# Reading and turning x inside the first expert's program, on one Trainium2 core

## The chip, the core and the metric

The kernel runs on one core of a Trainium2 chip. Its engines are TensorE (PE in the profile; PEld is its weight load), VectorE (DVE), ScalarE (ACT), GpSimd (POOL) and SyncE (SP). SP and ACT can both issue DMAs, each into a queue of its own (q1 is SP's, q10 is ACT's); the core's 16 DMA engines serve both. The metric is the device time of one launch in microseconds.

## What is computed

The program is a chain of four blocks on x (32 sequences of 64 tokens, width 256, so N = 2048 tokens): a gated sum over nine SwiGLU experts, an attention on that sum, five routed experts with two shared ones, and a second attention with four routed experts. The change touches the start of the first block alone. Cut to that block:

```python
# h = x; E, D, F = 8, 256, 1024; g are gating probabilities, Sg, Su, Sd the shared expert
g = jnp.einsum('bsd,edf->ebsf', h, Wg)
u = jnp.einsum('bsd,edf->ebsf', h, Wu)
expert_outs = jnp.einsum('ebsf,efd->ebsd', jax.nn.silu(g) * u, Wd)
# result: shared gate * shared expert + (1 - shared gate) * sum over e of gate[e] * expert_outs[e]
```

## The kernel before, in words

**Two programs.** `load_inputs` is a program of its own with a block of instructions for each engine. SP loads the table of constants (`const`, whose first 128 columns are the identity), x in four quarters into `x_tok`, and six small inputs with many tiny rows (`load_small`: gates, types, a bias, a threshold). ACT issues the first expert's weights: gate and up (`stage_up`, 1 MB each) and down (`stage_dn`, 1 MB). PE turns x: tokens lie in the partitions of `x_tok`, features in those of `xT`; 32 transposes of 128x128 go through the eight PSUM banks, four to a bank. ACT writes the rounded copy `x_hi`, DVE (and for every second bank ACT) the plain copy `xT`, DVE the remainder `x_lo = x - x_hi`. POOL sets the sum `sumT` to zero. At the end DVE waits for the small inputs and prepares the gates (`not_shared` L2039 to `type_sel` L2049). Then `sem.give_back()` clears the semaphores and all engines meet at a barrier. Only then comes `ffn`.

**The expert program.** `ffn` runs nine experts over four tiles of 512 tokens (`TT` = 4) and eight slices of 128 hidden features (`FC` = 8), so an expert has 32 steps (`STEPS`), counted by `st`. The first expert is written out, those between run in a loop on every engine. For a step PE does an up step (`up_step`, L269, here called U0, U1, ...: gate and up, 12 matmuls of 128x512) and a down step (`down_step`, L285, here D0, D1, ...: 6 matmuls). PE runs U two steps ahead: U0, U1, then U2, D0, U3, D1 and so on. Every product is made of three matmuls on rounded parts (hi*hi, hi*lo, lo*hi), so weights are split too: ACT rounds a slice (`round_up` L318, `round_down` L326), POOL subtracts (`cond_w_lo` L239, `cond_d_lo` L245). For the first expert ACT rounds all eight slices of up and then all eight of down before it does anything else.

**Between U and D.** ACT computes `silu` (L337), DVE multiplies it into `h` (L406), ACT rounds `h` one step later (`h_hi`, L331), DVE makes the remainder `h_lo` (L377). D of step st needs that `h_lo` and the down slice. Two pairs of banks (0 to 3) hold the products of U, banks 4 to 7 the sums of D, 6 and 7 from the second token tile on. After each token tile DVE's `take` multiplies the sum by the gate into `part` and adds it to `sumT` (L394, L397). Hooks of a `Beside` object let other work join; here `WeightsBeside` only adds the loads and the split of the next block's weights late in the program.

**Queues.** Every engine runs its own instructions strictly in order, and waits are on semaphores. SP issues the next expert's weights when all eight slices of `w_lo` (then of `d_lo`) are made.

Of the kernel before, what the change touches and what calls it, by code (L numbers as in the profile page):

```python
# [27 lines left out]
SLOT = 256  # L28

# [57 lines left out]
class ExpertStage:  # L87


    def __init__(self, nc, ctx, tag, ups):  # L90
        self.up = ctx.enter_context(nc.sbuf_tensor(f"{tag}_stage_up", [P, ups, KC, F], F32))
        self.down = ctx.enter_context(nc.sbuf_tensor(f"{tag}_stage_dn", [P, FC, D], F32))
        self.up_loaded = ctx.enter_context(nc.semaphore(f"{tag}_up_loaded"))
        self.dn_loaded = ctx.enter_context(nc.semaphore(f"{tag}_dn_loaded"))

    def load_up(self, sp, sources):
        for j, src in enumerate(sources):
            sp.dma_start(self.up[:, j], src).then_inc(self.up_loaded, 16)

# [4 lines left out]
class Beside:  # L104


    def sync_early(self, sp):
        pass
# [19 lines left out]
    def sync_late(self, sp):  # L128
        pass


class WeightsBeside(Beside):


    def __init__(self, weights):
        self.sync_late, self.scalar_late, self.gpsimd_late = weights.load, weights.round, weights.split
# [35 lines left out]
def ffn(nc, m, tag, swiglu, groups, gate, targets, x_hi, x_lo, stage, beside):  # L172
# [19 lines left out]
    with ExitStack() as s:  # L192
# [16 lines left out]
        with nc.Block() as block:  # L209
# [21 lines left out]
            def _(pool):  # L231
                def split(e):
# [14 lines left out]
                split(0)  # L247
                if n == 2:
# [7 lines left out]
            def _(pe):  # L256
# [31 lines left out]

                for st in range(2):
                    up_step(0, st)  # L290
                def expert(e, first):
                    for st in range(STEPS):
                        if first and st == FC:
# [16 lines left out]
            def _(act):  # L310
                def round_up(e, i):


                    if i == 0:
# [18 lines left out]
                def expert(e, first, last):  # L333
                    for st in range(STEPS):
# [30 lines left out]
            def _(dve):  # L365
# [4 lines left out]
                dve.nop().then_inc(gated, 2 * KC)  # L370

# [11 lines left out]
                def take(e, tt, target):  # L383
# [3 lines left out]
                    for c in range(KC):  # L387
# [4 lines left out]
                        if not (isinstance(e, int) and e == 0 and tt == 0):  # L392
                            dve.wait_ge(summed, KC * (TT * e + tt - 1) + c + 1)
# [5 lines left out]
                def expert(e, first, target, before):  # L399
                    for st in range(STEPS):  # L400
# [11 lines left out]
                        else:  # L412
                            split(e, st)
                        if first and st == FC + 1:
# [1558 lines left out]
def load_inputs(nc, m, x, x_hi, x_lo, stage, up, down):  # L1973

    sem = StageSemaphores(nc, "load")
    const_loaded, turned, taken, rounded = sem("const_loaded"), sem("x_turned"), sem("x_taken"), sem("x_rounded")
    small_loaded, gated, copied = sem("small_loaded"), sem("gated"), sem("x_copied")
    QT = 4
    x_loaded = [sem(f"x_loaded{q}") for q in range(QT)]
    with ExitStack() as s:  # L1980
        x_tok = s.enter_context(nc.sbuf_tensor("x_tok", [P, NP, D], F32))
        BANKS = 8
        with nc.Block() as block:
            @block.sync
            def _(sp):
                sp.dma_start(m.const[:], m.consts_dram).then_inc(const_loaded, 16)
                rows = x.rearrange("b t d -> (b t) d").rearrange("(i p) d -> p i d", p=P)
                for q in range(QT):
                    i = slice(q * NP // QT, (q + 1) * NP // QT)
                    sp.dma_start(x_tok[:, i], rows[:, i]).then_inc(x_loaded[q], 16)  # L1990
                m.load_small(sp, small_loaded)

            @block.gpsimd
            def _(pool):
                pool.memset(m.sumT[:], 0.0)
                pool.memset(m.minus_one[:], -1.0)
                pool.memset(m.zero_row[:], 0.0)

            @block.tensor
            def _(pe):  # L2000
                pe.wait_ge(const_loaded, 16)
                for i in range(NP // 2):
                    if i % 2 == 0:
                        pe.wait_ge(x_loaded[i // 2], 16)
                    if i >= BANKS:
                        pe.wait_ge(taken, i - BANKS + 1)
                    for j in range(2):
                        for c in range(KC):
                            ins = pe.transpose(m.bank[i % BANKS][:, (c * 2 + j) * P:(c * 2 + j + 1) * P],
                                               x_tok[:, 2 * i + j, c * P:(c + 1) * P], m.ident)  # L2010
                    ins.then_inc(turned, 1)

            @block.scalar
            def _(act):
                stage.load_up(act, up)
                stage.load_down(act, down)
                for i in range(NP // 2):
                    tok = slice(i * 2 * P, (i + 1) * 2 * P)
                    bank = m.bank[i % BANKS].rearrange("p (c t) -> p c t", c=KC)
                    act.wait_ge(turned, i + 1)  # L2020
                    act.activation(x_hi[:, :, tok], bank, ACT.Copy).then_inc(rounded, 1)
                    if i % 2 == 1:
# [187 lines left out]
```

## Time and profile before

| | |
|---|---|
| runs of the kernel | 2348.88 us median of 3 (2348.33 to 2353.54) |
| the profiled execution | 2349.1 us, of it a span of 2347.3 us from the first instruction to the last |
| mean granted TensorE clock | 0.943 of full speed |
| PE busy in the span | 2109.5 us, 90% |
| ACT / DVE / POOL busy | 907.1 / 1223.0 / 764.7 us |
| first matmul of the experts | at 40.82 us |
| last matmul of the ninth expert | at 1226.03 us |
| DMA moved | 135.74 MB, 58 GB/s over the span |

A row of the timeline gives the start, the duration, the engine, line, operation, destination and sources of one instruction or of several alike in a row (xN); in brackets how long the engine had been idle before it, and whose work ended that idle time. Times of a stretch are microseconds from the start of the span. A granted clock of 1.00 is 2.4 GHz on TensorE, 0.50 is 1.2 GHz.

### The profile page before, as it was taken

Reading aid. Unit: us, or ns where it says so; the run is one execution under the profiler, and the core shown is the slowest. Engines: PE = TensorE matmul, PEld = TensorE weight load, DVE = VectorE, ACT = ScalarE, POOL = GpSimd, SP = SyncE. Lnnn points to the kernel's source line nnn. Section 1 sums busy time; section 2 is a strip of 40 time slices with the busy share of each in tenths; the row PEclk is TensorE's granted clock in tenths of the full one; section 3 lists DMA queues with packets and bytes.
Section 4 is the critical chain, followed back from the end, with each engine's and each line's share of the span. In section 5 each row is a group of like instructions: output and inputs, shape, how many; then the busy total and the mean of one; then the engine's idle time right before and its main releaser. Section 6 shows DMA issues by size and latency. Waiting matters only on the chain. (4 is left out here: it accounts for less than half of the span.)

```text
span 2347.3 us, 32471 instructions
## 1 busy us (share of the span) xinstructions
PE 2109.5 (90%) x11748; PEld 1791.1 (76%) x11748; DVE 1223.0 (52%) x1989; ACT 907.1 (39%) x1780; POOL 764.7 (33%) x844
## 2 busy tenths in 40 slices
PE   3999999999999999999988797999897468967998
PEld 2888888888888888888877676788797157847997
DVE  2343344433344334443348894423784866657886
ACT  3233332324232332324222696132553223445554
POOL 3021020303020110203003595020783475507885
PEclk7999999999999999999997798999998688978999
DMA  3001010101001010200003002200463031036661
GB/s 124 30 0 55 1 54 0 54 0 47 7 2 51 0 54 0 78 0 0 1 1 72 24 37 102 94 9 1 154 198 97 18 72 40 38 107 225 206 202 58
DMA packets 84957, 135.74 MB, mean 58 GB/s; under 512 B 9678, under 2 KB 63312, under 8 KB 84880
## 3 DMA queue, kind: packets, MB, share of 16 engines
q1 hardware_dynamic: 78368, 118.72, 15.8%
q0 software_dynamic: 4928, 12.86, 1.6%
q10 hardware_dynamic: 1584, 3.15, 0.4%
q8 instruction: 47, 0.77, 0.1%
q14 instruction: 30, 0.25, 0.0%
HBM read 106.91 MB, written 12.06 MB: 51 GB/s over the span
## 5 line engine op out<-in xcount | busy, mean ns | idle before, releaser
L406 DVE TENSOR_TENSOR cond_h<-cond_silu,ps 128x512 f32<-128x512 f32 x288 | 197.9, 687 | 712.6 <-ACT cond_silu L337 709.0
L337 ACT ACTIVATE cond_silu<-ps 128x512 f32<-128x512 f32 x288 | 172.2, 598 | 793.7 <-PE ps L269 793.7
L269 PE MATMUL ps<-a_x_hi,cond_w_hi 128*128 128x512 f32 x1152 | 450.3, 391 | 20.6 <-POOL cond_w_lo L239 20.6
L269 PE MATMUL ps<-a_x_lo,cond_w_hi 128*128 128x512 f32 x1152 | 450.0, 391 | 0.0
L269 PE MATMUL ps<-a_x_hi,cond_w_lo 128*128 128x512 f32 x1152 | 449.8, 390 | 0.0
L239 POOL TENSOR_TENSOR cond_w_lo<-cond_stage_up,cond_w_hi 128x256 fp32r<-128x256 f32 x144 | 108.1, 771 | 869.4 <-ACT cond_w_hi L318 869.4
L269 PEld LDWEIGHTS ps<-a_x_hi,cond_w_hi 128*128 128x128 f32 x1152 | 217.3, 189 | 66.0 <-POOL cond_w_lo L239 20.8
L269 PEld LDWEIGHTS ps<-a_x_lo,cond_w_hi 128*128 128x128 f32 x1152 | 217.3, 189 | 45.1
L269 PEld LDWEIGHTS ps<-a_x_hi,cond_w_lo 128*128 128x128 f32 x1152 | 217.2, 189 | 45.1
L285 PE MATMUL ps<-cond_h_hi,cond_d_hi 128*128 128x512 f32 x576 | 224.8, 390 | 5.3 <-POOL cond_d_lo L245 4.5
L285 PE MATMUL ps<-cond_h_hi,cond_d_lo 128*128 128x512 f32 x576 | 224.8, 390 | 0.0
L285 PE MATMUL ps<-cond_h_lo,cond_d_hi 128*128 128x512 f32 x576 | 224.7, 390 | 0.0
L377 DVE TENSOR_TENSOR cond_h_lo<-cond_h,cond_h_hi 128x512 fp32r<-128x512 f32 x288 | 202.9, 705 | 0.1
L331 ACT ACTIVATE cond_h_hi<-cond_h 128x512 fp32r<-128x512 f32 x288 | 179.7, 624 | 0.3 <-DVE cond_h L406 0.3
L285 PEld LDWEIGHTS ps<-cond_h_hi,cond_d_hi 128*128 128x128 f32 x576 | 108.3, 188 | 28.5 <-POOL cond_d_lo L245 4.9
L1678 POOL TENSOR_TENSOR moe_w_lo<-moe_stage_up,moe_w_hi 128x512 fp32r<-128x512 f32 x88 | 114.9, 1321 | 38.6 <-ACT moe_w_hi L1779 37.8
L285 PEld LDWEIGHTS ps<-cond_h_hi,cond_d_lo 128*128 128x128 f32 x576 | 108.3, 188 | 22.5
L285 PEld LDWEIGHTS ps<-cond_h_lo,cond_d_hi 128*128 128x128 f32 x576 | 108.3, 188 | 22.4
L1731 PE MATMUL ps<-moe_x_hi,moe_w_hi 128*128 128x256 f32 x352 | 101.3, 288 | 13.9 <-DVE moe_x_lo L1832 13.9
L380 DVE SCALAR_TENSOR_TENSOR dense_h_lo<-ps,dense_h_hi 128x512 fp32r<-128x512 f32 x64 | 44.2, 692 | 122.6 <-ACT dense_h_hi L343 122.6
L1678 POOL TENSOR_TENSOR typed_w_lo<-typed_stage_up,typed_w_hi 128x256 fp32r<-128x256 f32 x88 | 69.0, 804 | 97.5 <-ACT typed_w_hi L1779 96.7
L1731 PE MATMUL ps<-moe_x_lo,moe_w_hi 128*128 128x256 f32 x352 | 100.7, 286 | 0.0
(357 smaller groups left out, 4396.7 us busy)
## 6 DMA issues: line engine op xcount, KB each, us to landing
moe_stage_up<-in_L_ffn_expert_wv SPq DMA_DIRECT2D x22, 1024.0 KB, 8.8
typed_stage_up<-in_L_cond_wi SPq DMA_DIRECT2D x11, 1024.0 KB, 5.0
typed_stage_dn<-in_L_cond_wo SPq DMA_DIRECT2D x11, 1024.0 KB, 5.4
moe_stage_dn<-in_L_ffn_expert_proj SPq DMA_DIRECT2D x11, 1024.0 KB, 5.6
cond_stage_up<-in_L_cond_Wg SPq DMA_DIRECT2D x7, 1024.0 KB, 4.9
cond_stage_up<-in_L_cond_Wu SPq DMA_DIRECT2D x7, 1024.0 KB, 7.0
cond_stage_dn<-in_L_cond_Wd SPq DMA_DIRECT2D x7, 1024.0 KB, 5.3
hyp_v_now<-hyp_v_blk SPq DMA_DIRECT2D x16, 272.0 KB, 2.3
```

What stands on the lines that cost most here:

```text
L239: ins = pool.tensor_tensor(w_lo[:, j, :, c], stage_up[:, j, :, c], w_hi[:, j, :, c], ALU.subtract)
L269: ins = pe.matmul(up_ps[st % 2][j], w[:, j, k, fs], x[:, k, tok], start=(i == 0), stop=(i == 3 * KC - 1))
L285: ins = pe.matmul(y_ps[tt % 2][c], w[:, f, cs], x[:, st % HB], start=(f == 0 and i == 0), stop=(f == FC - 1 and i == 2))
L331: act.activation(h_hi[:, st % HB], h[:, st % 2], ACT.Copy).then_inc(h_rounded, 1)
L337: act.activation(silu[:, st % 2], up_ps[st % 2][0], ACT.Silu).then_inc(act_done, 1)
L377: dve.tensor_tensor(h_lo[:, st % HB], h[:, st % 2], h_hi[:, st % HB], ALU.subtract).then_inc(h_ready, 1)
L380: dve.scalar_tensor_tensor(h_lo[:, st % HB], up_ps[st % 2][0], 0.0, h_hi[:, st % HB], ALU.max, ALU.subtract).then_inc(h_ready, 1)
L406: dve.tensor_tensor(h[:, st % 2], silu[:, st % 2], up_ps[st % 2][1], ALU.mult).then_inc(up_free, 1)
L1678: pool.tensor_tensor(w_lo[:, :, :, fs(f)], stage_up[:, q, :, :, fs(f)], w_hi[:, :, :, fs(f)], ALU.subtract).then_inc(up_ready, 1)
L1731: ins = pe.matmul(up_ps[f % UB][j], w[:, j, k, fs(f)], x[:, q, k], start=(i == 0), stop=(i == 3 * KC - 1))
```

## The change

`load_inputs` is gone as a program. Its work hangs on the hooks of `ffn` as `StartBeside`:

- SP loads the identity alone, the four quarters of x, the rest of the constants, then the small inputs. The raw rows of x lie in the memory of `sumT`, which nobody else needs yet.
- ACT issues the weights in five pieces: gate and up of the first two slices (`HEAD` = 2), their other six slices, down.
- PE turns the first quarter of x, waits until its copies are made, and starts with U0. The other three quarters are turned ahead of U3, U5 and U7 (steps 1, 3, 5), always through banks 6 and 7. ACT and DVE do their copies of a quarter in the same steps.
- For the first expert ACT rounds slice 0 of up, does its part of the first quarter, rounds slices 1 and 2, and rounds the rest one slice of up and one of down in each of the first steps.
- `sumT` isn't set to zero as a whole: the first expert's `take` writes it (one DVE operation in place of two), and only its last quarter is cleared by POOL, since that quarter is taken in the loop. The gates are prepared by DVE in step 9.
- One clearing of semaphores with its barrier goes with `load_inputs`.

```diff
+    def sync_early(self, sp):
+        m = self.m
+        sp.dma_start(m.const[:, 0:P], m.consts_dram[:, 0:P]).then_inc(self.ident_loaded, 16)
+        for q in range(self.QT):
+            i = slice(q * NP // self.QT, (q + 1) * NP // self.QT)
+            sp.dma_start(self.x_tok[:, i], self.rows[:, i]).then_inc(self.x_loaded[q], 16)
+        sp.dma_start(m.const[:, P:], m.consts_dram[:, P:]).then_inc(self.const_loaded, 16)
+        m.load_small(sp, self.small_loaded)
+    def scalar_start(self, act):
+        self.stage.load_up_head(act, self.up)
+        self.stage.load_up_rest(act, self.up)
+        self.stage.load_down(act, self.down)
+    def gpsimd_clear(self, pool):
+        pool.wait_ge(self.turned, NP // 2)
+        for c in range(KC):
+            pool.memset(self.m.sumT[:, c, N - TW:], 0.0).then_inc(self.cleared, 1)
+    def tensor_tile(self, pe, t):
+        if t == 0:
+            pe.wait_ge(self.ident_loaded, 16)
+        pe.wait_ge(self.x_loaded[t], 16)
+        for i in range(2 * t, 2 * t + 2):
+            bank, _ = self.place(i)
+            if i >= 2:
+                pe.wait_ge(self.taken, i - 1)
+            for j in range(2):
+                for c in range(KC):
+                    ins = pe.transpose(bank[:, c, j * P:(j + 1) * P], self.x_tok[:, 2 * i + j, c * P:(c + 1) * P], self.m.ident)
+            ins.then_inc(self.turned, 1)
+    def tensor_ready(self, pe, t):
+        pe.wait_ge(self.taken, 2 * (t + 1))
+    def scalar_tile(self, act, t):
+        for i in range(2 * t, 2 * t + 2):
+            bank, tok = self.place(i)
+            act.wait_ge(self.turned, i + 1)
+            act.activation(self.x_hi[:, :, tok], bank, ACT.Copy).then_inc(self.rounded, 1)
+            if i % 2 == 1:
+                act.activation(self.m.xT[:, :, tok], bank, ACT.Copy).then_inc(self.copied, 1)
...
@@ (PE, ffn)
+                beside.tensor_tile(pe, 0)
+                beside.tensor_ready(pe, 0)
                 for st in range(2):
                     up_step(0, st)
                 def expert(e, first):
                     for st in range(STEPS):
+                        if first and st in (1, 3, 5):
+                            beside.tensor_tile(pe, (st + 1) // 2)
+                        if first and st % FC == FC - 2 and st + 2 < STEPS:
+                            beside.tensor_ready(pe, (st + 2) // FC)
...
@@ (ACT, ffn)
+                        if first and beside.paced:
+                            if st + HEAD + 1 < FC:
+                                round_up(0, st + HEAD + 1)
+                            if st < FC:
+                                round_down(0, st)
+                            if st in (1, 3, 5):
+                                beside.scalar_tile(act, (st + 1) // 2)
...
-                for i in range(FC):
-                    round_up(0, i)
-                for i in range(FC):
-                    round_down(0, i)
+                beside.scalar_start(act)
+                if beside.paced:
+                    round_up(0, 0)
+                    beside.scalar_tile(act, 0)
+                    for i in range(1, HEAD + 1):
+                        round_up(0, i)
...
@@ (DVE, ffn, take)
-                        if not (isinstance(e, int) and e == 0 and tt == 0):
-                            dve.wait_ge(summed, KC * (TT * e + tt - 1) + c + 1)
+                        if isinstance(e, int) and e == 0:
+                            dve.tensor_tensor(target[:, c, tok].rearrange(v, t=T), y_ps[tt % 2][c].rearrange(v, t=T),
+                                              gate(e, tt), ALU.mult).then_inc(gated, 1)
+                            continue
+                        dve.wait_ge(summed, KC * (TT * e + tt - 1) + c + 1)
```

`vector_tile` is DVE's counterpart of `scalar_tile`: it copies the even bank into `xT` and subtracts for `x_lo`, as in `load_inputs`; step 31 of DVE waits for POOL's clearing.

## Rows read from the trace of the kernel before

**Rows 1.** Timeline, the first 41 us: start us, us, engine, line, operation.
```profile
1.18 6.71 SPq L1990 DMA_DIRECT2D x_tok<-in_x  x4
...
11.57 1.94 PE L2009 MATMUL ps<-const,x_tok 128*128 128x128 f32 x8 [11.57 <-DMA x_tok<-in_x]
...
13.93 1.50 DVE L2035 TENSOR_TENSOR a_x_lo<-ps,a_x_hi 128x512 fp32r<-128x512 f32 x2
14.04 0.59 ACT L2023 ACTIVATE xT<-ps 128x512 f32<-128x512 f32 x1
...
17.08 3.13 PE L2009 MATMUL ps<-const,x_tok 128*128 128x128 f32 x16 [0.57 <-DMA x_tok<-in_x]
...
36.30 0.18 DVE L2039 TENSOR_SCALAR not_shared<-gate_cond 128x32 f32<-128x32 f32 x1 [13.54 <-DMA threshold<-in_L_attn_threshold]
...
38.55 5.01 ACT L318 ACTIVATE cond_w_hi<-cond_stage_up 128x256 fp32r<-128x256 f32 x16 [16.90 <-PEq L84]
39.35 5.55 POOL L239 TENSOR_TENSOR cond_w_lo<-cond_stage_up,cond_w_hi 128x256 fp32r<-128x256 f32 x8 [34.84 <-ACT cond_w_hi L318]
...
40.82 0.79 PE L269 MATMUL ps<-a_x_hi,cond_w_hi 128*128 128x512 f32 x1 [20.61 <-POOL cond_w_lo L239]
```

**Rows 2.** Timeline, 50 to 96 us, the first down steps.
```profile
50.08 0.69 DVE L406 TENSOR_TENSOR cond_h<-cond_silu,ps 128x512 f32<-128x512 f32 x1 [1.36 <-ACT cond_silu L337]
...
50.68 5.81 DVE L377 TENSOR_TENSOR cond_h_lo<-cond_h,cond_h_hi 128x512 fp32r<-128x512 f32 x1
...
53.18 2.76 POOL L245 TENSOR_TENSOR cond_d_lo<-cond_stage_dn,cond_d_hi 128x256 fp32r<-128x256 f32 x4
...
56.59 0.47 PE L285 MATMUL ps<-cond_h_hi,cond_d_hi 128*128 128x512 f32 x1 [4.54 <-POOL cond_d_lo L245]
...
62.40 0.39 PE L285 MATMUL ps<-cond_h_hi,cond_d_hi 128*128 128x512 f32 x1
...
95.04 0.39 PE L285 MATMUL ps<-cond_h_hi,cond_d_hi 128*128 128x512 f32 x1
```

**Rows 3.** Windows of 1 us: busy time per engine, then PEclk, DMA share, GB/s.
```profile
46.00:47.00 1.00, 1.00 (x4) 0.77 (x4) 0.00 (x0) 0.98 (x2) 1.00 (x3) 0.60 0.00 0
...
57.00:58.00 1.00, 1.00 (x4) 0.76 (x3) 0.82 (x2) 0.00 (x0) 0.00 (x0) 0.52 1.01 406
...
60.00:61.00 1.00, 1.00 (x4) 0.80 (x4) 0.00 (x0) 0.00 (x0) 0.00 (x0) 0.77 1.00 367
```

**Rows 4.** DMA view by stretch: 0 to 5, 5 to 10 and 20 to 36.3 us.
```profile
DMA packets 278, 0.99 MB, mean 198 GB/s; under 512 B 16, under 2 KB 16, under 8 KB 278
...
DMA packets 859, 2.01 MB, mean 402 GB/s; under 512 B 31, under 2 KB 481, under 8 KB 859
...
q10 hardware_dynamic: 450, 1.59, 78.4%
q1 hardware_dynamic: 409, 0.42, 23.9%
...
q1 hardware_dynamic: 1975, 0.01, 5.5%
```

**Rows 5.** Transposes by source line (ns min/median/max), and windows over two of them.
```profile
L2009 PE MATMUL ps<-const,x_tok x32: 272/421/477, 11.6 to 19.9; 128*128 128x128 f32 x32
...
L1920 PE MATMUL ps<-const,c_back_y x32: 420/422/473, 1806.5 to 1814.5; 128*128 128x128 f32 x32
...
1445.50:1449.10 3.60, 3.47 (x32) 3.48 (x32) 2.39 (x3) 3.49 (x5) 0.00 (x0) 1.00 0.50 196
...
1810.00:1812.00 2.00, 2.00 (x11) 2.00 (x10) 0.00 (x0) 1.09 (x2) 0.00 (x0) 0.50 1.09 357
...
11.00:12.00 1.00, 0.43 (x2) 0.46 (x3) 0.00 (x0) 0.00 (x0) 0.00 (x0) 1.00 1.09 350
```

**Rows 6.** Timeline of one step in which the next expert's weights are split.
```profile
161.82 0.69 DVE L377 TENSOR_TENSOR cond_h_lo<-cond_h,cond_h_hi 128x512 fp32r<-128x512 f32 x1
...
162.32 1.48 POOL L239 TENSOR_TENSOR cond_w_lo<-cond_stage_up,cond_w_hi 128x256 fp32r<-128x256 f32 x2 [2.60 <-ACT cond_w_hi L318]
```

More of the change, by code:

```diff
@@ L104, with gpsimd_start, tensor_left, vector_tile @@
 class Beside:
+    paced = False
     def sync_early(self, sp):
+        pass
+    def scalar_start(self, act):
+        pass
+    def gpsimd_start(self, pool):
+        pass
+    def tensor_tile(self, pe, t):
+        pass
+    def tensor_ready(self, pe, t):
+        pass
+    def tensor_left(self, pe):
+        pass
+    def scalar_tile(self, act, t):
+        pass
+    def vector_tile(self, dve, t):
+        pass
+    def gpsimd_clear(self, pool):
+        pass
+    def vector_cleared(self, dve):
         pass
@@ L231, in _ @@
             def _(pool):
+                beside.gpsimd_start(pool)
                 def split(e):
@@ L247, in _ @@
                 split(0)
+                beside.gpsimd_clear(pool)
                 if n == 2:
@@ L292, in expert @@
                     for st in range(STEPS):
+                        if first and st in (1, 3, 5):
+                            beside.tensor_tile(pe, (st + 1) // 2)
+                        if first and st % FC == FC - 2 and st + 2 < STEPS:
+                            beside.tensor_ready(pe, (st + 2) // FC)
+                        if first and st == FC:
+                            beside.tensor_left(pe)
                         if first and st == FC:
@@ L311, in round_up @@
                 def round_up(e, i):
-                    if i == 0:
+                    if beside.paced and isinstance(e, int) and e == 0:
+                        if i == 0:
+                            act.wait_ge(stage.head_loaded, 16 * ups)
+                        elif i == HEAD:
+                            act.wait_ge(up_loaded, 16 * ups)
+                    elif i == 0:
                         act.wait_ge(up_loaded, 16 * ups * (e + 1))
@@ L370, in _ @@
                 dve.nop().then_inc(gated, 2 * KC)
+                if gate is not None:
+                    dve.nop().then_inc(summed, KC * (TT - 1))
+                beside.vector_tile(dve, 0)
                 def split(e, st, offset=0):
@@ L413, in expert @@
                             split(e, st)
+                        if first and st in (1, 3, 5):
+                            beside.vector_tile(dve, (st + 1) // 2)
+                        if first and st == STEPS - 1:
+                            beside.vector_cleared(dve)
                         if first and st == FC + 1:
@@ L2114, in program @@
                 sg, su, sd = one(a["L0_cond_Sg"]), one(a["L0_cond_Su"]), one(a["L0_cond_Sd"])
-                load_inputs(nc, m, a["x"], x_hi, x_lo, stage, (up(wg)(0), up(wu)(0)), down(wd)(0))
+                start = StartBeside(nc, m, s, a["x"], x_hi, x_lo, stage, (up(wg)(0), up(wu)(0)), down(wd)(0), hyp)
                 groups = [(E_COND, lambda e: (up(wg)(e), up(wu)(e)), down(wd)),
@@ L2119, in program @@
                     "p o b -> p (o b)").unsqueeze(2).to_broadcast([P, BT, T])
-                ffn(nc, m, "cond", True, groups, gate, [m.sumT, m.sumT], x_hi, x_lo, stage, WeightsBeside(hyp))
+                ffn(nc, m, "cond", True, groups, gate, [m.sumT, m.sumT], x_hi, x_lo, stage, start)
             attention(nc, m, "hyp", True, m.sumT, m.xT, hyp)
```

143 lines of the change are left out of this document (69 added, 74 removed).

## The prediction

> **What bounds the kernel now.** I read the table of the profile first: PE is busy for 90% of the span, so what counts is where it isn't. The windows show it: over the nine experts, from 62.40 us on, a step takes (95.04 - 62.40) / 8 = 4.08 us for 18 matmuls [rows 2], 0.2267 us each, back to back. Nothing done beside PE there is worth anything. The hole lies ahead of it. Up to 40.82 us PE does nothing but 32 transposes [rows 1].
>
> The timeline of the start says what that hole waits for. The first quarter of x is there at 11.5 us, the last is turned at 20.2 us (17.08 + 3.13). But the old program ends only when DVE has its small inputs, at 36.30 us, after 13.54 us of idling; then come 1.5 us of gates, the clearing and the barrier, and ACT starts rounding weights at 38.55 us, though their last bytes were there long before. POOL follows at 39.35, PE at 40.82 [rows 1]. The DMA view tells why the small inputs are late: 1975 packets with 0.01 MB fill SP's queue from 20 to 36.3 us [rows 4].
>
> The second loss is just behind. U0, U1, U2 and then 4.54 us of idling before D0 at 56.59 us [rows 2]. The row names POOL's `d_lo` as releaser, but POOL had ended at 55.94 (53.18 + 2.76); what ended at 56.49 was DVE's `h_lo`, which took 5.81 us in place of 0.69 [rows 2, 6]. It started at 50.68, while POOL went from one subtraction to the next without a gap, and ended when POOL had. `h` at 50.08, which reads PSUM, took its 0.69 in the same stretch [rows 2]. So POOL's unbroken work holds up a DVE subtraction of two SBUF tensors.
>
> The third is the clock. At 40.82 us the matmuls run at the 1.2 GHz level; the window of 46 to 47 us shows 0.60, so the rise came at 46.8, 6.0 us after the first matmul. After the idling it falls at 57.0 (0.52 in that window) and is back at 60.46 (0.77 in its window), 3.9 us after D0's start [rows 3]. Check: from 40.82 to D1 at 62.40 are 21.58 us; U0 to U3 and D0 are 54 matmuls, 12.24 us at full clock; 4.54 us were idle; the 4.8 us left are half of the 9.4 us spent at the lower clock. So a microsecond at 1.2 GHz costs half a microsecond.
>
> **The anchor.** Behind the change the steps after T3 (the last quarter) are what they were, and so is the rest of the program. I therefore date D1, at 62.40 us before, and add what is inserted later.
>
> **When x and the weights arrive.** Between 5 and 10 us ACT's queue had 450 packets and SP's 409, but 1.59 MB against 0.42 [rows 4]: the queues take turns by packet, and ACT's were 4 KB (rows of F), SP's 1 KB (rows of x). This is what the smaller head buys. Before, the first quarter ended with SP's packet 640 (128 of constants, 512 of x); with 640 of ACT's (512 of 4 KB, 128 of 1 KB) that is 3.19 MB. By 10 us 3.0 MB had moved, so the last byte moved at about 10.5 us, and PE started at 11.5: a lag of 1 us. Now packet 640 of SP (128 of identity, 512 of x) goes with 512 of ACT's of 1 KB and 128 of 3 KB, in all 1.51 MB: 0.99 by 5 us, the rest at 402 GB/s by 6.3, landed at 7.3; for smaller packets at the start I take 7.4. The bound above is 11.5 us, as before. By the same count the heads are there at about 6, the other six slices of up at 11.1 and down at 17.3 us.
>
> ACT must issue five DMAs of 2048 packets before it can round. SP's four issues of x took 6.71 us [rows 1], so its last one was held up while the queue was full. If ACT is held until 7.9 us like SP, slice 0 of `w_lo` is made by 10.1 us (0.7 on ACT, 1.48 on POOL [rows 6]), still ahead of U0. So nothing is charged.
>
> **T0 and U0.** From the first transpose (11.57) to the end of the second `x_lo` (13.93 + 1.50) were 3.86 us [rows 1]. That chain is unchanged, two banks suffice for it, and PE waits for all of it: U0 at 7.4 + 3.9 = 11.3 us. Is T0 as slow as before? The granted clock of that stretch reads 1.00, but the transposes took 421 ns, like those of `c_back` at a granted 0.50 (420 to 422), and not 272, as the last of the sixteen [rows 5]. The row for the first microseconds doesn't show the level; the durations do, and they say 1.2 GHz. So U0 starts at the lower clock, and I take the mean of the two rises seen, 4.95 us after the first matmul: 2.5 us lost. Bounds: nothing, if T0 has raised it, and 3.4 (half of 6.8, the longer spell and one more microsecond).
>
> **U0 to D1.** Work 12.24 us. Slices 1 and 2 of up: ACT is done with its part of T0 at 10.5 (14.04 + 0.59 is 3.1 after the transposes' start [rows 1]) and rounds them until 11.9; POOL follows until 14.1; U1 starts at about 16.5, U2 at 19.2. Down lands at 17.3, ACT rounds its slice 0 after slice 3 of up, by 18.2; `d_lo` is made at 20.0 (1.48 for `w_lo`, 0.7 for `d_lo` [rows 6, 2]); D0 comes at 21.9. That is 1.9 us of slack, the smallest here. The 4.54 us of idling go: POOL now works in bursts of 2.2 us per step, paced by ACT, as for later experts, where `h_lo` gets in first and takes 0.69 [rows 6].
>
> T1 is 8 transposes at full clock: 32 took 3.48 us [rows 5], so 0.9 us. Behind it ACT does three copies (the second must wait for the first 0.6, not for PE), then `silu`, then `h_hi`; DVE `h_lo`. From the start of T1: 0.5 until the first four are turned, 1.8 for the copies, 1.1 for `silu` and `h_hi` back to back, 0.7 for `h_lo`: 4.1 us. PE needs 0.9 + 2.7 (T1, U3) before it asks for it: 0.5 us of waiting. Bounds: none, or 2.2 (a burst of POOL ahead of `h_lo`).
>
> **The sum.** D1 at 11.3 + 12.24 + 2.5 + 0.9 + 0.5 = 27.4 us. T2 and T3 add 1.4 each, 2.8. So 62.40 - 30.2 = 32.2 us are saved. The other edits cost nothing: six of DVE's adds and POOL's 3.5 us of zeroing weren't on PE's path; the gates (1.5 us) stand in step 9 of DVE, at 27.4 + 2.8 + 8 x 4.08 = 63 us, 27 us after the small inputs landed before, and a step leaves DVE some 2.7 us; SP's next loads are for weights wanted 100 us later. If the step's cover were gone the gates would cost their 1.5 us once. Span 2347.3 - 32.2 = 2315.1, time 2316.9 with the profiled execution's 1.8 us around it; the median of the runs is 0.2 lower: 2316.7 us.
>
> **Rivals.**
> 1. *The first quarter comes no earlier.* The small pieces might share the DMA engines no better than the large ones. X at 11.5 us again: 4.1 more, 2320.8 us. Against it the packet counts. Chance 0.12.
> 2. *POOL starves `h_lo` after all.* The 5.81 us show that it can. If `h_lo` falls into POOL's burst in each of the eight paced steps, it comes 2.2 us late against 0.6 of slack (`h_lo` 21.1, D0 21.7 to 21.9): 8 x 1.6 = 12.8, 2329.5 us. The Trainium skill, page "SBUF — State Buffer", section "Who interferes with whom", says that a Vector instruction with two SBUF inputs waits until the GpSimd instruction that came first has finished; that would be 0.7 us here and lie in the slack. The row of 5.81 us, eight of POOL's instructions long, speaks against its price, not against its mechanism. Chance 0.06.
> 3. *Slower: the clock doesn't stay up in the first expert,* because of the transposes and waits put between the matmuls. Each microsecond at 1.2 GHz costs a half, so it decides from 64 us (8 of these slow steps) on; over the 31 steps after D1 it would cost 126 us, 2443 us. Against it: the falls seen followed 4.54 us of idling, the new gaps are 0.5 us, or 1.4 if transposes count as idling, and from 60.46 on the clock held. The Trainium skill, page "TensorE: Matmul & The Clock Gate", section "Part 4: PE-mode transpose", says that transposes don't count as busy for the clock, which would feed this rival. The trace doesn't agree: of the sixteen transposes from 17.08 the whole took 3.13 us where eight alone took 1.94 [rows 1], so the clock rose while nothing but transposes ran. Chance 0.03.
> 4. *No change.* The wait for the small inputs moves to step 9 and holds DVE there. For the whole gain they would have to land at 95 us. Chance 0.02.
>
> **Numbers.** My forecast has 0.77. 0.2% is 4.7 us, about what a measurement of this kernel can tell from no change. Rivals 1 and 2 are faster too: faster 0.95, same 0.02, slower 0.03. Range: below, no loss to the clock (2.5), no waits behind the quarters (1.5) and 1.5 for the clock's falls in the later blocks, which come as they fall (the three runs differ by 5.2 us): 2311. Above, rival 1 and a good half of rival 2: 2328.
>
> **What would show it.** First transpose at 7.4 us (11.5: rival 1); first matmul of 128x512 at 11.3; D0 at about 22 without 4 us of idling; PE idle under 1 us behind T1, T2, T3; `h_lo` at 0.69 throughout (longer: rival 2); PEclk 1.00 from 17 us on (rival 3); `not_shared` at about 63 us without a DMA as releaser; the last matmul of the ninth expert at 1226.03 - 32.2 = 1193.8; and everything behind it shifted by that. The prediction is wrong if PE waits for the down weights at D0, if ACT sits in its DMA issues past 9 us, or if a later block answers the shift with a different clock.

## The result and the profile after

The changed kernel takes 2320.13 us (median of 4 runs, 2318.53 to 2323.47) where the one before took 2348.89 (median of 4, 2348.33 to 2353.54): 0.9875 of it, with a 95% interval of 0.9863 to 0.9888. The forecast was 2316.7, range 2311 to 2328; the time is inside it and 3.4 us above the forecast. The profiled execution took 2319.53 us.

The page of the changed kernel: its span, the busy time of the engines, and PE's granted clock in 40 slices. The falls of the clock are all in the later half, in blocks that nothing edits.

```profile
span 2317.7 us, 32452 instructions
...
PE 2104.6 (91%) x11748; PEld 1784.8 (77%) x11748; DVE 1213.9 (52%) x1983; ACT 906.6 (39%) x1780; POOL 763.5 (33%) x845
...
PEclk9999999999999999999997898999997688978999
```

The timeline of the changed kernel, 7 to 60 us (start, length, engine, line, operation, in brackets the idling before it and its releaser). L236 are the transposes, L411 the up matmuls, L427 the down matmuls. T0 to T3 below are the turnings of the four quarters of x.

```profile
6.97 0.72 ACT L473 ACTIVATE cond_w_hi<-cond_stage_up 128x256 fp32r<-128x256 f32 x2 [2.22 <-DMA cond_stage_up<-in_L_cond_Wu]
7.27 1.94 PE L236 MATMUL ps<-const,sum 128*128 128x128 f32 x8 [7.27 <-DMA sum<-in_x]
...
11.18 0.80 PE L411 MATMUL ps<-a_x_hi,cond_w_hi 128*128 128x512 f32 x1 [1.98 <-DVE a_x_lo L261]
...
12.99 0.72 ACT L473 ACTIVATE cond_w_hi<-cond_stage_up 128x256 fp32r<-128x256 f32 x2 [2.06 <-DMA cond_stage_up<-in_L_cond_Wu]
...
16.90 0.47 PE L411 MATMUL ps<-a_x_lo,cond_w_hi 128*128 128x512 f32 x1
17.20 0.40 PE L411 MATMUL ps<-a_x_hi,cond_w_lo 128*128 128x512 f32 x1
...
19.26 0.42 ACT L481 ACTIVATE cond_d_hi<-cond_stage_dn 128x256 fp32r<-128x256 f32 x1 [1.34 <-DMA cond_stage_dn<-in_L_cond_Wd]
...
22.21 0.39 PE L427 MATMUL ps<-cond_h_hi,cond_d_hi 128*128 128x512 f32 x1
...
23.58 1.04 PE L236 MATMUL ps<-const,sum 128*128 128x128 f32 x8
24.21 1.09 ACT L249 ACTIVATE a_x_hi<-ps 128x512 fp32r<-128x512 f32 x2 [2.49 <-PE ps L236]
24.37 0.48 PE L411 MATMUL ps<-a_x_hi,cond_w_hi 128*128 128x512 f32 x1
...
25.19 0.61 ACT L251 ACTIVATE xT<-ps 128x512 f32<-128x512 f32 x1
...
25.66 0.62 ACT L492 ACTIVATE cond_silu<-ps 128x512 f32<-128x512 f32 x1
...
28.07 0.47 PE L427 MATMUL ps<-cond_h_hi,cond_d_hi 128*128 128x512 f32 x1 [0.71 <-DVE cond_h_lo L549]
...
38.10 0.47 PE L427 MATMUL ps<-cond_h_hi,cond_d_hi 128*128 128x512 f32 x1 [0.73 <-DVE cond_h_lo L549]
...
47.34 1.20 DVE L549 TENSOR_TENSOR cond_h_lo<-cond_h,cond_h_hi 128x512 fp32r<-128x512 f32 x1
...
48.69 0.47 PE L427 MATMUL ps<-cond_h_hi,cond_d_hi 128*128 128x512 f32 x1 [1.21 <-DVE cond_h_lo L549]
...
1196.10 0.39 PE L427 MATMUL ps<-cond_h_hi,cond_d_lo 128*128 128x512 f32 x1
```

I put the time in the order of the prediction's terms. "Block end" below is the start of the ninth expert's last matmul: 1226.03 before, 1196.10 after, 29.93 us earlier. What comes behind it took 1121.3 us of the span before (2347.3 - 1226.03) and 1121.6 after: the gain is all in the start.

- The first 128x512 matmul moves from 40.82 [rows 1] to 11.18: 29.64 saved.
- From it to D1 it was 21.58 us [rows 2], and is 16.89 (28.07 - 11.18): 4.69 saved. D0 comes 11.03 us after the first matmul with no idling of note ahead of it; before there were 4.54 us [rows 2].
- From D1 on the pieces cost: D1 to D3 is 10.03 us, two steps of 4.08 and 1.87 more; D3 to D5 10.59, so 2.43 more; 0.10 behind that. Together 4.40 given back.

29.64 + 4.69 - 4.40 = 29.93.

At 16.90 the matmuls follow each other by 0.30 us and from 17.20 by 0.24, down from 0.43 before: the clock rose at about 17.1, 5.9 us after the first matmul. It stays up across the three pieces of transposes.

### The profile page after: what moved, and what is told of

Its sections match the earlier page's. It is cut to its first block and busy times, and to the rows that moved or that the text cites. A ratio compares the mean times of both kernels' runs of the same rounds, so it can differ in the third digit from the quotient of the medians.

```text
span 2317.7 us, 32452 instructions
## 1 busy us (share of the span) xinstructions
PE 2104.6 (91%) x11748; PEld 1784.8 (77%) x11748; DVE 1213.9 (52%) x1983; ACT 906.6 (39%) x1780; POOL 763.5 (33%) x845
## 5 line engine op out<-in xcount | busy, mean ns | idle before, releaser
L411 PE MATMUL ps<-a_x_hi,cond_w_hi 128*128 128x512 f32 x1152 | 449.8, 390 | 2.0 <-DVE a_x_lo L261 2.0
L411 PE MATMUL ps<-a_x_lo,cond_w_hi 128*128 128x512 f32 x1152 | 449.2, 390 | 0.0
L411 PE MATMUL ps<-a_x_hi,cond_w_lo 128*128 128x512 f32 x1152 | 449.1, 390 | 0.0
L411 PEld LDWEIGHTS ps<-a_x_hi,cond_w_hi 128*128 128x128 f32 x1152 | 217.0, 188 | 47.3 <-DVE a_x_lo L261 2.4
L411 PEld LDWEIGHTS ps<-a_x_hi,cond_w_lo 128*128 128x128 f32 x1152 | 216.9, 188 | 45.2
L411 PEld LDWEIGHTS ps<-a_x_lo,cond_w_hi 128*128 128x128 f32 x1152 | 217.0, 188 | 44.9
L427 PE MATMUL ps<-cond_h_hi,cond_d_hi 128*128 128x512 f32 x576 | 224.4, 390 | 3.4 <-DVE cond_h_lo L549 3.4
L427 PE MATMUL ps<-cond_h_hi,cond_d_lo 128*128 128x512 f32 x576 | 224.1, 389 | 0.0
L427 PE MATMUL ps<-cond_h_lo,cond_d_hi 128*128 128x512 f32 x576 | 224.1, 389 | 0.0
L427 PEld LDWEIGHTS ps<-cond_h_hi,cond_d_hi 128*128 128x128 f32 x576 | 108.1, 188 | 27.3 <-issue 2.2
L427 PEld LDWEIGHTS ps<-cond_h_hi,cond_d_lo 128*128 128x128 f32 x576 | 108.1, 188 | 22.5
L427 PEld LDWEIGHTS ps<-cond_h_lo,cond_d_hi 128*128 128x128 f32 x576 | 108.1, 188 | 22.3
```

Of the source, the lines that this page charges most:

```text
L411: ins = pe.matmul(up_ps[st % 2][j], w[:, j, k, fs], x[:, k, tok], start=(i == 0), stop=(i == 3 * KC - 1))
L427: ins = pe.matmul(y_ps[tt % 2][c], w[:, f, cs], x[:, st % HB], start=(f == 0 and i == 0), stop=(f == FC - 1 and i == 2))
```

## Experiments

Most differences here are a few us, and the unedited blocks behind the experts vary by as much (last section). So each kernel is read twice: by its median and ratio, and by the block end of its profiled execution. Each ratio is to the kernel before, measured again beside the kernel in question.

### `gates_late`: the kernel before, small inputs' wait moved to step 9

Only the gates' preparation moves, out of the loading program and into the first expert.

```diff
-                dve.wait_ge(small_loaded, 16 * m.n_small)
-                (not_shared, gate_cond, neg_b_sur, type_in, type_sel)
+    def vector_early(self, dve):          # DVE, step 9
+        dve.wait_ge(m.small_loaded, 16 * m.n_small)
+        (the same instructions)
```

> The kernel before, with one part of the change alone: DVE prepares the gates in step 9 of the first expert and no longer at the end of the loading program. If the tiny rows of the small inputs hold the start, the loading program ends with DVE's last remainder of x at 22.8 us in place of 37.8, U0 starts 15.0 us earlier, at 25.8, the stall before D0 stays as it is, and the time is 2348.9 - 15.0 = 2333.9 us. Rival: the wait only moves to something else in the loading program (down weights, the barrier), then 2348.9.

Measured: 2335.84 us (2331.36 to 2342.59, 4 runs), ratio 0.9936 [0.9919, 0.9952]; block end 1211.98, 14.05 earlier. The timeline of `gates_late`:

```profile
25.70 0.79 PE L283 MATMUL ps<-a_x_hi,cond_w_hi 128*128 128x512 f32 x1 [5.26 <-POOL cond_w_lo L253]
...
34.92 6.46 DVE L391 TENSOR_TENSOR cond_h_lo<-cond_h,cond_h_hi 128x512 fp32r<-128x512 f32 x1
...
38.09 2.75 POOL L259 TENSOR_TENSOR cond_d_lo<-cond_stage_dn,cond_d_hi 128x256 fp32r<-128x256 f32 x4
...
41.49 0.76 PE L299 MATMUL ps<-cond_h_hi,cond_d_hi 128*128 128x512 f32 x1 [4.75 <-POOL cond_d_lo L259]
```

So nearly half of the gain is one wait. The second stall came along whole: `h_lo` took 6.46 us, D0 waited 4.75, and the matmul behind it shows the lower clock's 0.76 again. It hangs on POOL's run, not on the date. The first matmul comes 15.12 us earlier and D0 15.10, as expected; 1.1 of it is gone by D1 (48.40), because the granted clock stayed at 0.50 until 47.37, 5.9 us after D0's start, where it had been 3.9 before.

### `pool_gap`: the kernel before, POOL pauses once for `h_lo`

```diff
+    if isinstance(e, int) and e == 0 and tag == "cond" and k == 3:
+        pool.wait_ge(h_ready, 3)
```

> The kernel before, with one wait added: POOL makes down's slice 3 of the first expert only when DVE has made its first h_lo. If POOL's unbroken run is what held DVE's h_lo for 5.8 us and with it D0, h_lo takes 0.7 to 1.4 us, D0 starts at about 52.1 in place of 56.6, the clock does not fall a second time (1.7 us more), and the time is 2348.9 - 6.2 = 2342.7 us. Rival: D0 waits for POOL's d_lo, as the row of the matmul names it; then D0 stays at 56.6 or comes later, 2348.9 or above.

Measured: 2343.8 us (2339.2 to 2349.79, 9 runs), ratio 0.9981 [0.9968, 0.9994]; block end 1219.51, 6.5 earlier. The timeline of `pool_gap`:

```profile
49.67 1.43 POOL L239 TENSOR_TENSOR cond_w_lo<-cond_stage_up,cond_w_hi 128x256 fp32r<-128x256 f32 x2
...
50.62 1.03 DVE L379 TENSOR_TENSOR cond_h_lo<-cond_h,cond_h_hi 128x512 fp32r<-128x512 f32 x1
...
51.80 0.73 POOL L247 TENSOR_TENSOR cond_d_lo<-cond_stage_dn,cond_d_hi 128x256 fp32r<-128x256 f32 x1 [0.70 <-DVE cond_h_lo L379]
...
53.34 1.13 DVE L379 TENSOR_TENSOR cond_h_lo<-cond_h,cond_h_hi 128x512 fp32r<-128x512 f32 x1
```

A pause of 0.70 us on POOL is worth 6.5 us: `h_lo` takes 1.03, ending 0.55 after the POOL instruction it met (49.67 + 1.43). PE has no 4.54 us of idling and the clock doesn't fall a second time. This shows the cause of the second loss, and its price.

### `whole_up`: the changed kernel, up weights loaded in one piece each again

`load_up_head` and `load_up_rest` are replaced by the old `load_up` (two DMAs of 4 KB rows); ACT waits for all of it at slice 0.

> The changed kernel with gate and up weights loaded whole (rows of 4 KB), not in a head and a rest. If the two queues take turns by packet, the first quarter of x ends with SP's packet 640 and 512 of ACT's of 4 KB: 2.82 MB in place of 1.51, so the first transpose comes at 10.6 us in place of 7.3 and the time is 3.3 us longer, 2323.4 us. Rival: the pieces do not matter, transpose at 7.3, 2320.1; or with full weights first it comes at 11.5, as before the change, 2324.3.

Measured: 2322.95 us (2320.47 to 2324.26, 4 runs), ratio 0.9884 [0.9867, 0.99]; block end 1199.59, 3.49 after that of the changed kernel. The timeline of `whole_up`:

```profile
10.96 1.94 PE L235 MATMUL ps<-const,sum 128*128 128x128 f32 x8 [10.96 <-DMA sum<-in_x]
```

x is asked for as early and in the same pieces as in the changed kernel, and comes 3.7 us later (10.96 against 7.27). All that differs are the packets that it shares the DMA engines with, four times as long. That is the prediction's count of packets, and it speaks against rival 1's mechanism: the size of the pieces does matter.

### `late_copies`: the changed kernel, copies of T1 to T3 behind the `silu` and `h_hi` of the step

```diff
+                            if st in (2, 4, 6):          # behind silu and h_hi of the step
+                                beside.scalar_tile(act, st // 2)
-                            if st in (1, 3, 5):
-                                beside.scalar_tile(act, (st + 1) // 2)
```

and the same for DVE's tile.

> The changed kernel with ACT's and DVE's copies of quarters 1, 2, 3 in steps 2, 4, 6, behind that step's silu and h_hi, not in steps 1, 3, 5 ahead of the next silu; PE's order is the same. If D1, D3 and D5 wait because silu sits behind the copies on ACT, the 0.86, 0.88 and 1.3 us between the last matmul ahead of them and their first go to zero: 3.0 us less, 2317.1 us. Rival: they wait because h_lo is held by POOL; then the gaps stay and so does the time, 2320.1.

Measured: 2316.66 us (2314.86 to 2318.94, 4 runs), ratio 0.9863 [0.9846, 0.9879]; block end 1192.86, 3.24 before that of the changed kernel. No wait is left behind T1, T2 and T3. The timeline of `late_copies`, T1, the first matmul of U3, and D1:

```profile
23.82 1.04 PE L236 MATMUL ps<-const,sum 128*128 128x128 f32 x8
...
24.61 0.48 PE L411 MATMUL ps<-a_x_hi,cond_w_hi 128*128 128x512 f32 x1
...
27.43 0.39 PE L427 MATMUL ps<-cond_h_hi,cond_d_hi 128*128 128x512 f32 x1
```

D1 follows U3's first matmul by 2.82 us, where it was 3.70 (28.07 - 24.37). In the changed kernel `silu` of step 2 started at 25.66, behind two `x_hi` (24.21 to 25.30) and `xT` (25.19 to 25.80), though its matmuls were done at about 22.2. DVE's `h` likewise stood behind two `x_lo` (25.45 to 26.73). The order on ACT and DVE is the cause of these waits, and not POOL.

### `unpaced`: the changed kernel, ACT rounds all sixteen slices ahead of the first `silu`

```diff
-                    for i in range(1, HEAD + 1):
+                    for i in range(1, FC):
                         round_up(0, i)
+                    for i in range(FC):
+                        round_down(0, i)
```

and the roundings inside the steps are left out. It was meant to give POOL its unbroken run back.

> The changed kernel, with ACT rounding all slices of the first expert's weights before its first silu, as the kernel before did; loads, quarters of x and everything else as changed. If POOL's unbroken run starves DVE, POOL runs without a gap from about 20 to 31 us, the first h_lo ends only then, D0 starts at 31 in place of 22.2, the clock falls, and the time is 10 to 12 us longer, about 2331 us. Rival, by which a DVE instruction waits for one of POOL's at most: D0 waits only for ACT, which has its 16 slices done at 22 us, starts at about 25.5, and the time is 2323.6 us. Second rival: pacing is worth nothing, 2320.1.

Measured: 2327.04 us (2325.87 to 2329.57, 4 runs), ratio 0.9902 [0.9882, 0.9922]; block end 1203.65, 7.55 later than the changed kernel. The timeline of `unpaced`:

```profile
20.16 2.56 ACT L481 ACTIVATE cond_d_hi<-cond_stage_dn 128x256 fp32r<-128x256 f32 x8 [2.13 <-DMA cond_stage_dn<-in_L_cond_Wd]
...
20.66 0.73 POOL L386 TENSOR_TENSOR cond_d_lo<-cond_stage_dn,cond_d_hi 128x256 fp32r<-128x256 f32 x1 [2.81 <-ACT cond_d_hi L481]
...
24.04 1.08 ACT L492 ACTIVATE cond_silu<-ps 128x512 f32<-128x512 f32 x2
...
25.57 0.77 PE L411 MATMUL ps<-a_x_hi,cond_w_hi 128*128 128x512 f32 x1 [6.41 <-DVE cond_h L579]
...
26.12 1.29 DVE L547 TENSOR_TENSOR cond_h_lo<-cond_h,cond_h_hi 128x512 fp32r<-128x512 f32 x1
26.82 1.17 POOL L386 TENSOR_TENSOR cond_d_lo<-cond_stage_dn,cond_d_hi 128x256 fp32r<-128x256 f32 x1
```

The size lies between the 10 to 12 us expected and the rival's 3.5; the reason is the rival's. POOL ran from 20.66 to 32.1 without a pause of its own, but `h_lo` took 1.29: it waited for the POOL instruction that ended at 26.86 and came through 0.55 later, while the next one of POOL took 1.17 in place of 0.73. Nothing was starved. The loss is ACT's: its sixteen roundings waited for the down weights until 20.16, the first `silu` came at 24.04, and PE idled 6.41 us for a free bank. In that idling the clock fell, and it came back only at 29.59; D0 started at 30.27. So pacing is needed for ACT's sake, and "POOL's unbroken work holds up DVE" is too broad.

### `pool_more` and `gap_early`: how long is `h_lo` held, and what lets it in?

Both start from the kernel before. `pool_more` adds twelve subtractions of 128x256 on POOL into a scratch buffer, behind the first split. `gap_early` lets POOL pause once earlier, and run through afterwards.

```diff
+                    for i in range(12):                                   # pool_more
+                        pool.tensor_tensor(more[:, i], m.const[:, 0:D], m.const[:, 0:D], ALU.subtract)
+                            if isinstance(e, int) and e == 0 and tag == "cond" and k == 1:   # gap_early
+                                pool.wait_ge(act_done, 1)
```

> The kernel before with twelve more subtractions of 128x256 on POOL right behind the first expert's split (into scratch, 8.4 us more of POOL without a gap). If DVE's first h_lo is held until POOL has a gap, it ends at about 65 us in place of 56.5 and D0 with it. Rival: it is held for as many of POOL's instructions as were waiting ahead of it, about eight, and ends at 56.5 to 57 as before.

> The kernel before with POOL made to wait once, at down's slice 1, for the first silu (done at 47.9), so that it has run without a gap for 3 us and not for 11 when h_lo(0) comes at 50.6; it then goes on without a gap for 5 us more. If any unbroken run of POOL starves DVE, h_lo takes 5 to 7 us as before. Rival: the length of the run before it matters; h_lo gets in after one of POOL's instructions, 0.9 to 1.3 us, and D0 starts at 52, as in pool_gap.

Measured, one run each: `pool_more` 2357.77 us, D0 at 63.54 (6.95 later than before), block end 1233.68, 7.65 later; `gap_early` 2344.32 us, D0 at 51.63 (4.96 earlier), block end 1219.32, 6.71 earlier. In both the clock rose sooner than before, 3.8 and 3.1 us after the first matmul in place of 6.0, so the ends alone don't measure the hold. The rows do. The timeline of `pool_more`:

```profile
49.72 13.71 DVE L382 TENSOR_TENSOR cond_h_lo<-cond_h,cond_h_hi 128x512 fp32r<-128x512 f32 x1
...
56.01 6.87 POOL L252 TENSOR_TENSOR cond_more<-const 128x256 f32<-128x256 f32 x12
...
63.54 0.77 PE L290 MATMUL ps<-cond_h_hi,cond_d_hi 128*128 128x512 f32 x1 [11.57 <-issue]
...
1233.68 0.39 PE L290 MATMUL ps<-cond_h_hi,cond_d_lo 128*128 128x512 f32 x1
```

That of `gap_early`:

```profile
48.01 0.73 POOL L247 TENSOR_TENSOR cond_d_lo<-cond_stage_dn,cond_d_hi 128x256 fp32r<-128x256 f32 x1 [1.07 <-ACT cond_silu L339]
...
48.70 1.95 POOL L239 TENSOR_TENSOR cond_w_lo<-cond_stage_up,cond_w_hi 128x256 fp32r<-128x256 f32 x2
...
49.36 0.69 DVE L379 TENSOR_TENSOR cond_h_lo<-cond_h,cond_h_hi 128x512 fp32r<-128x512 f32 x1
...
55.24 3.27 POOL L247 TENSOR_TENSOR cond_d_lo<-cond_stage_dn,cond_d_hi 128x256 fp32r<-128x256 f32 x4
...
57.21 0.70 DVE L379 TENSOR_TENSOR cond_h_lo<-cond_h,cond_h_hi 128x512 fp32r<-128x512 f32 x1
```

There is no cap of some number of instructions: in `pool_more` the one DVE instruction is held for 13.71 us, until POOL's last subtraction ended at 62.88, and ends 0.55 us later. In the kernel before it ended 0.55 behind POOL too (56.49 and 55.94 [rows 2]), in `gates_late` 0.54 (41.38 and 40.84). With a pause on POOL that ended 1.35 us ahead of it, `h_lo` isn't held at all, though POOL then runs on to 58.5. The next two of `gap_early` get in as well, 5.1 and 9.2 us into that run of POOL's (53.13, 0.85 us; 57.21, 0.70 us).

### `warm`, `down_head`, `warm_down`: what else limits the start

All three start from `late_copies`. `warm` lets PE multiply zeros (8 matmuls of 128x256 ahead of T0, 3 behind it, into a bank that is cleared by its next user) to have the clock up. `down_head` loads two slices of down right behind the heads of up, and the rest last. `warm_down` does both.

```diff
+            pe.matmul(m.bank[0][:, 0:D], m.zero_row[:, 0:P], m.zero_row[:, 0:D], start=True, stop=True)
+        act.dma_start(s.down[:, 0:HEAD], self.down[:, 0:HEAD]).then_inc(s.dn_head_loaded, 16)
```

> The kernel late_copies, with eight matmuls of zeros on PE ahead of the first quarter and three behind its transposes (into a bank that U0 overwrites). If PE is at 1.2 GHz at the start though the granted clock reads 1.00, these raise it: T0 takes 1.0 us in place of 1.94 and U0's matmuls follow at 0.227 us in place of 0.427. But D0 then waits for the down weights, which land at 19 to 20 us, and for the copies behind them on ACT: D0 at about 22.2 as in late_copies, gain 0.3 us at most, 2316.5. Rival: the row is right, T0 and U0 stay as slow as they are for another reason; the same time with nothing changed in them. Second rival: down is not the next limit, D0 comes 3 us earlier, 2313.7.

> The kernel late_copies, with down loaded in two pieces: its first two slices right behind the heads of gate and up, the other six last. With PE at the lower clock as before, U2 ends at 22.2 and D0 follows, since down's slice 0 is ready long before: no gain, 2316.7 us, or 0.2 less. If the extra 256 KB ahead of up's rest delays slice 2 of w_lo past U2's start at 16.8 us, it is up to 1 us slower.

> warm and down_head together, on late_copies. If the clock at the start and the landing of down are limits one behind the other, only both together bring it: U0, U1, U2 at full clock from 11.1 us on end at 19.3, D0 follows at 19.3 to 19.9, 2.5 to 3.0 us less than late_copies: 2314.0 us. Rival: slice 2 of up, whose rest comes 1 us later, holds U2: gain 1 to 1.5 us, 2315.4.

| kernel | median us (runs) | ratio | block end | D0 |
|---|---|---|---|---|
| `warm` | 2317.65 (4) | 0.9861 [0.9842, 0.9881] | 1193.54 | 21.46 |
| `down_head` | 2317.74 (4) | 0.9864 [0.9845, 0.9883] | 1192.55 | 22.14 |
| `warm_down` | 2319.55 (4) | 0.9871 [0.9852, 0.9889] | 1192.57 | 22.18 |

None gains on `late_copies` (1192.86) by more than 0.3. The timeline of `warm`:

```profile
7.19 1.06 PE L243 MATMUL ps<-const,sum 128*128 128x128 f32 x8 [0.77 <-DMA sum<-in_x]
...
10.43 0.50 PE L420 MATMUL ps<-a_x_hi,cond_w_hi 128*128 128x512 f32 x1 [0.87 <-DVE a_x_lo L270]
...
19.06 0.42 ACT L490 ACTIVATE cond_d_hi<-cond_stage_dn 128x256 fp32r<-128x256 f32 x1 [3.03 <-DMA cond_stage_dn<-in_L_cond_Wd]
...
21.46 0.76 PE L436 MATMUL ps<-cond_h_hi,cond_d_hi 128*128 128x512 f32 x1 [2.13 <-issue]
```

T0's eight transposes take 1.06 us here and 1.94 in the changed kernel: there they ran at 1.2 GHz, as the prediction had read from the durations [rows 5]. PE had nothing more to do at 19.33 (21.46 - 2.13), 2.9 us before D0 in the changed kernel, and stood waiting until 21.46, by which time the clock had fallen (0.76). What let it go was `h_lo` (20.67 to 21.35), whose `h_hi` (19.86) stood on ACT behind the rounding of the down weights, which landed at 19.06. In `warm_down`, where down's head is early, the rest of up is late instead: it landed at 15.77, its rounding stood ahead of the first `silu` (17.81), and D0 came at 22.18.

### `x_held` and `weights_first`: the later quarters of x held back

`x_held` is `down_head` with one wait in SP's queue; `weights_first` is `x_held` and `warm` together. The first expectation below is that of `x_held`; its "the same" means `weights_first`, whose expectation comes second.

```diff
             sp.dma_start(self.x_tok[:, i], self.rows[:, i]).then_inc(self.x_loaded[q], 16)
+            if q == 0:
+                sp.wait_ge(self.stage.up_loaded, 32)
```

> The same without the matmuls of zeros. If the clock is the limit as soon as the weights are early, U0 still runs at 1.2 GHz, D0 comes at 22.1 as in late_copies and down_head, and the ninth expert ends at 1192.5: no gain, 2316.7 to 2317.7 us. Rival: the early weights alone bring it, 1190.

> warm_down with one wait more: SP issues quarters 1 to 3 of x only when gate and up of the first expert have landed. In warm_down the rest of up landed at 15.8 us and silu(0) stood behind its rounding on ACT, so U2 waited. If the later quarters of x are what slows the weights (they take half of the packets), up's rest lands at about 11 us (2.94 MB in place of 3.55), U0 to U2 run at full clock without a gap from 10.8 on, D0 starts at about 19.0 in place of 22.2, and the ninth expert ends 3 us earlier than in late_copies, at 1189.8; 2313.6 us. Rival: PE then waits for T1, whose quarter comes late, or for something else on ACT; no gain, 1192.6.

Measured: `x_held` 2314.46 us (2312.33 to 2316.38, 4 runs), ratio 0.9851 [0.9832, 0.9869], block end 1191.72, D0 at 21.27. `weights_first` 2313.23 us (2310.57 to 2316.34, 5 runs), ratio 0.9843 [0.9827, 0.9858], block end 1189.18, D0 at 18.80. DMA of the changed kernel from 6 to 13 us, then of `weights_first` from 6 to 12 (packets, MB, share of 16 engines for the two queues; q10 is ACT's, q1 SP's):

```profile
q10 hardware_dynamic: 770, 1.80, 66.8%
q1 hardware_dynamic: 894, 0.89, 37.9%
```

```profile
q10 hardware_dynamic: 1258, 2.28, 99.9%
q1 hardware_dynamic: 63, 0.05, 3.1%
```

With x's later quarters held back, the rest of up is there at 11.80 (12.99 in the changed kernel, 15.02 in `down_head`). Of the 1.14 us by which `x_held`'s block ends ahead of `late_copies`, 0.8 can be the clock, which rose 3.9 us after the first matmul there and 5.5 in `late_copies`. Only with the clock, down's head and x's place mended together does the block end move by much: 3.7 us ahead of `late_copies`. That down's head is needed for it is argued from `warm` and not shown: no run has the other two without it. This is the best kernel of the study, 6.9 us ahead of the changed one by the block end, and 0.9843 against 0.9875 of the time before. The two ratios were not measured side by side, and their intervals just don't overlap.

## Why the prediction was right, step by step

**What bounds it** held. The rest of the program took what it had taken (1121.6 and 1121.3 us), so the gain is the start's alone, as said.

**x and the weights.** The first quarter was predicted at 7.4 and came at 7.27; the count of packets behind it was tested by `whole_up` (predicted 10.6, came at 10.96). The later landings were off: up's rest at 12.99 for 11.1, down at 19.26 for 17.3. Between 6 and 13 us SP had 894 packets to ACT's 770, not one for one, at 384 GB/s, not 402. It cost nothing in this kernel: `d_lo` of slice 0 was made at 20.49 (19.75 and 0.74), 1.7 us ahead of D0, where 1.9 was said, because POOL was done with its `w_lo` (19.43) before down was rounded. ACT wasn't held in its DMA issues either: its five ended at 3.44 us.

**U0** came at 11.18 for 11.3, and at the lower clock, as read.

**The clock.** The mean of two spells, 4.95 us, was taken; it took 5.9, so 2.95 us were lost for 2.5. That this term came out so near is partly luck: `pool_gap` and `gap_early` are the kernel before up to that point, and the clock rose 5.9 and 3.1 us after the first matmul there, for 6.0 before. The spell isn't a constant of the kernel; 0.4 us of error is small against its spread, of which half (1.4 us) goes into the time.

**The wait behind the pieces** is the term that was mis-sized most. T1, T2 and T3 with their waits were put at 1.4 us each and took 1.77, 1.87 and 2.43: 1.9 us in all. The working had the copies done 2.3 us after T1's start and PE waiting 0.5 us. ACT's were done at 25.80, 2.2 us after it, as said. What the working left out is DVE's own queue: two `x_lo` until 26.73, then `h` (26.65, 0.68), and only then `h_lo` (27.24 to 27.93). PE waited 0.71, 0.73 and 1.21, and the first matmul on either side of a gap took 0.08 more until the next could follow (24.37 to 24.68, 28.07 to 28.38). For T3 `h_lo` took 1.20 as well, behind a POOL instruction: a small part of rival 2. `late_copies` shows that the order of the copies is the cause: it gives back 3.24, of which 0.2 can be its clock.

**The sum.** For the block end 1193.8 was predicted and 1196.1 came. Of the 2.3: 1.9 for the pieces, 0.4 for the clock, 0.1 behind D5, less 0.1 for U0. The median is off by 3.4 (2320.13 for 2316.7), 1.1 more than the block end; that is within what the later blocks vary by.

**Step 9.** The gates stand there without a wait for a DMA, at 59.06 us; predicted at about 63. The row of the changed kernel:

```profile
59.06 0.18 DVE L267 TENSOR_SCALAR not_shared<-gate_cond 128x32 f32<-128x32 f32 x1
```

I had dated the step by PE's down step 9; DVE works ahead of PE and comes to it behind the `h_lo` that ended at 59.14, while PE is still two steps back (D7 at 56.95). That changes nothing else.

**Rival 1** (x no earlier): the first transpose says no. **Rival 2** (POOL starves `h_lo`): the mechanism is real, but not in this kernel: `h_lo` took 0.69, twice 0.87, and 1.20 and 1.11. The prediction's own reading of it was too broad. What the runs show: where POOL had worked 10.3 to 11.3 us without a break when the first `h_lo` came, DVE was held until POOL stopped (13.71, 6.46, 5.81 us; 1.03 in `pool_gap`, where POOL stopped at once). Where it had worked 5.5 us or less (the first two of `gap_early`, `unpaced`, the second `h_lo` of `pool_gap`), DVE got in after at most one POOL instruction, though POOL went on for up to 9 us more. The third `h_lo` of `gap_early` came 9.2 us into a run without a pause and wasn't held either; there DVE had been let in twice since the run began. So it is open what decides, the length of POOL's run or that DVE has not been let in since it began: no run has a first `h_lo` between 5.5 and 10.3 us. The Trainium skill, page "SBUF — State Buffer", section "Who interferes with whom", has DVE wait until the GpSimd instruction that came first has finished. The trace agrees where POOL's run was short, as where the second `h_lo` of `pool_gap` ended 0.55 us after the one POOL instruction that it met (54.47 and 53.92), and not where it was held for 5.81 to 13.71 us, over 8 of POOL's instructions and more. **Rival 3** (the clock stays down): it stayed up across all three pieces; the spacing of the matmuls behind T1 is 0.23 us from the second on. **Rival 4**: no wait in step 9.

**Where the gain is from.** Not waiting for the small inputs: 14.05, shown alone. POOL's hold on DVE and the clock's fall behind it: 6.5, shown alone. The remaining 9.4 of 29.93 were not taken apart by runs, but the rows place them. The first matmul comes 14.5 us earlier than in `gates_late` (25.70 and 11.18): 7.4 of these from the end of the first quarter's `x_lo` (15.28) to that of the last (22.68), which it no longer waits for; 4.15 because the first quarter is done sooner (15.28 and 11.13), most of it from the smaller pieces, by `whole_up`; 3.0 for the clearing, the barrier and the split of slice 0, which stood behind the last `x_lo`. Another 1.1 is the clock that `gates_late` lost behind D0. Against it stand 6.1 for the three pieces inside the steps.

## What to carry to other kernels

Don't end a loading stage with a wait for inputs of tiny rows: here they came last with 0.01 MB in all, and one semaphore wait moved to the place of first use was worth 14 us. If two queues load at the start, what is needed first should go in short rows together with short rows; and when a copy shares an engine with what feeds PE next, it belongs behind it. When such a start is tuned further, look for the next limit before the edit: here the clock, the down weights, the up weights and x lay close behind each other; `warm`, `down_head` and both together gave nothing beside `late_copies`, and with x held back as well they gave 3.7 us.

## What the runs showed of the hardware

- One DVE subtraction of two SBUF tensors was held for 13.71 us by some 20 short POOL subtractions issued back to back, and ended 0.55 us after POOL's last one (`pool_more`).
- The granted-clock row reads 1.00 in every window of the first 50 us of the changed kernel, though the matmuls lie 0.43 us apart until 17.1 (0.23 at full clock). Ahead of its first change the row doesn't show the level; only durations do (T0: 1.94 us, and 1.06 in `warm`).
- The blocks behind the experts, edited in none of the kernels, took 1120.8 to 1125.3 us in the profiled executions, but 1128.8 in `gates_late`. The granted clock there isn't the same from one execution to the next: 0.90 on average in `late_copies` (1120.8 us), 0.88 in `gates_late`. Single edits of 1 to 3 us can't be judged by one total time, and by the block end only when the date of the clock's rise is taken out.
- That date is not fixed. The clock rose 3.1 us after the first matmul in `gap_early`, 3.8 in `pool_more`, 3.9 in `x_held`, 4.6 in `gates_late`, 4.8 in `unpaced`, 5.4 in `whole_up`, 5.5 in `late_copies`, 5.7 in `down_head`, 5.9 in `pool_gap` and the changed kernel and 6.0 before, with the same code ahead of it in four of them (`gap_early`, `pool_gap`, `pool_more`, before).
